# A three-block decoder layer on one core: pairs of value groups in one PSUM bank, rows of maxima ahead of the next reductions, cross queries split by GpSimd, stack reads behind the rows

## The reference, cut to what matters

```python
# x, ctx: (4, 256, 128) float32; 16 heads of 8
x = x + self_attention(layernorm(x))        # rotary q and k, causal, softmax, @ Wo.T
x = x + cross_attention(layernorm(x), ctx)  # keys and values from ctx, softmax, @ W_proj + b_proj
x = x + moe(layernorm(x))                   # per batch row: mean over tokens -> router, top 2 of 8 experts,
                                            # gelu(h @ w1[e] + b1[e]) @ w2[e] + b2[e], weighted sum
```

## Time and profile before

| | |
|---|---|
| three runs | 200.36, 200.97, 201.46 us (median 200.97) |
| profiled execution | 200.95 us, of which the span in the trace is 199.2 us |
| busy: PE, PEld, DVE, ACT, POOL | 166.8, 116.1, 140.7, 104.8, 52.3 us |
| chain that ended last, by engine | PE 50%, DVE 19%, DMA 15%, SP's queue 5%, "issue" 4%, POOL 3% |
| granted TensorE clock, mean of the span | 0.947 |

### The profile page before, as it was taken

How to read it: one execution, slowest core, us unless ns; L and a number is a source line. 1 busy time by engine, 2 the same in 40 slices (tenths; PEclk the granted TensorE clock), 3 DMA queues, 4 the chain that set the end, 5 groups by cost and what they waited for, 6 DMA issues and landing times.

```text
span 199.2 us, 4411 instructions
## 1 busy us (share of the span) xinstructions
PE 166.8 (84%) x1500; PEld 116.1 (58%) x1508; DVE 140.7 (71%) x545; ACT 104.8 (53%) x222; POOL 52.3 (26%) x103
## 2 busy tenths in 40 slices
PE   0686195699599979989998998998998899799994
PEld 0343184485466755755764655654665556598984
DVE  2789299897347899799799889888968346525020
ACT  2132021257147656566566666766676657793451
POOL 7810005668800070030030030010115107126050
PEclk9999669589769999999999999999999999999999
DMA  5817660058227503322321321300340350170720
GB/s 150 238 35 175 164 173 18 3 148 184 70 82 196 184 25 104 110 69 58 109 82 49 98 95 35 90 0 3 113 130 3 100 143 0 17 224 26 229 66 26
DMA packets 23842, 19.05 MB, mean 96 GB/s; under 512 B 2364, under 2 KB 21820, under 8 KB 23100
## 3 DMA queue, kind: packets, MB, share of 16 engines
q1 hardware_dynamic: 22908, 17.79, 31.9%
q10 hardware_dynamic: 912, 0.98, 2.0%
HBM read 12.54 MB, written 2.49 MB: 75 GB/s over the span
## 4 chain that ended last, share of the span: by engine, by line
PE 50%; DVE 19%; DMA 15%; SPq 5%; issue 4%; POOL 3%; ACT 2%; POOLq 0%; DVEq 0%; ACTq 0%
PE psV L914 11%; PE psB L893 9%; PE psA L868 8%; DMA stackQ<-maxT 6%; DMA stackQ<-scratch 4%; DVE masked L623 4%; PE psA L958 4%; PE psM L923 3%; PE psA L975 3%; DMA stackK<-hid 3%; PE psV L975 3%; PE psM L933 3%; DVE stats L554 2%; DVE negmax L629 2%; SPq L402 2%
## 5 line engine op out<-in xcount | busy, mean ns | idle before, releaser
L753 ACT ACTIVATE E<-psB 128x512 f32<-128x512 f32 x112 | 62.3, 595 | 37.3 <-PE psB L893 15.7
L868 PE MATMUL psA<-stackK,stackQ 72*128 72x256 bf16 (+1 forms) x256 | 44.4, 277 | 11.8 <-DMA stackK<-hid 5.5
L893 PE MATMUL psB<-stackQ,stackK 74*128 74x256 bf16 (+1 forms) x256 | 42.2, 264 | 4.6 <-DMA stackQ<-maxT 3.8
L623 DVE CUSTOM_DVE_ANT_0 masked<-psA,row_mask 128x128 bf16<-128x128 f32 (+1 forms) x128 | 36.8, 352 | 11.8 <-PE psA L868 11.7
L629 DVE TENSOR_REDUCE negmax<-psA 128x2 f32<-128x512 f32 x64 | 39.7, 677 | 0.0
L868 PEld LDWEIGHTS psA<-stackK,stackQ 72*128 72x128 bf16 x256 | 23.0, 105 | 21.5 <-DMA stackQ<-scratch 8.6
L914 PE MATMUL psV<-E,V 128*9 128x256 f32 (+1 forms) x512 | 30.9, 359 | 0.2 <-ACT E L753 0.2
L893 PEld LDWEIGHTS psB<-stackQ,stackK 74*128 74x128 bf16 x256 | 22.0, 100 | 12.5 <-DMA stackQ<-maxT 5.6
L468 POOL TENSOR_SCALAR rstd<-mv 128x2 f32<-128x2 f32 x12 | 2.8, 236 | 89.1 <-DVE mv L558 88.9
L914 PEld LDWEIGHTS psV<-E,V 128*9 128x9 f32 x512 | 11.0, 90 | 14.4 <-issue 7.9
L761 ACT ACTIVATE oT<-psV 128x256 f32<-128x256 f32 x32 | 12.3, 384 | 7.9 <-PE psV L914 7.2
(11 more groups left out here) (111 smaller groups left out, 247.0 us busy)
## 6 DMA issues: line engine op xcount, KB each, us to landing
stackK<-scratch SPq DMA_DIRECT2D x18, 192.0 KB
stackQ<-hid SPq DMA_DIRECT2D x36, 64.0 KB
w1s<-w_dram SPq DMA_DIRECT2D x8, 258.0 KB, 2.8
w2s<-w_dram SPq DMA_DIRECT2D x8, 256.0 KB, 3.7
stackQ<-scratch SPq DMA_DIRECT2D x3, 576.0 KB
stackK<-hid SPq DMA_DIRECT2D x18, 64.0 KB
scratch<-hid SPq DMA_DIRECT2D x4, 192.0 KB, 3.7
scratch<-parts_ctx SPq DMA_DIRECT2D x4, 192.0 KB, 4.7
```

Of the source, the lines that this page charges most:

```text
L623: last = dve.tensor_tensor_reduce(out=masked[:, bank, i * keys:(i + 1) * keys], in0=scores[:, i, 0:keys], in1=row_mask[:, S - keys:S], sca ...
L753: act.activation(dst, psB[:, bank].rearrange("p (h q) -> p h q", h=dst.shape[1]), ACT.Exp, scale=SCALE).then_inc(b_taken, 1)
L868: last = pe.matmul(psA[:, bank, i * keys:(i + 1) * keys], stackQ[0:ROWS, b, h, t * P:(t + 1) * P], stackK[0:ROWS, b, h, 0:keys], start=Tru ...
L893: last = pe.matmul(psB[:, bank, i * n:(i + 1) * n], stackK[:, b, h, t * P:(t + 1) * P], stackQ[:, b, h, q0:S], start=(s == 1 or i == 0), s ...
```

## The change

1. **Values in pairs.** `V` has 27 columns for two heads: the first head's 8 values and a 1, nine zeros, the second head's 8 values and a 1. The heads are dealt out so that group 2k has the even ones of eight, group 2k + 1 the odd ones (`heads_of`). Each group's products use 18 of the 27 columns and add into the same 18 rows of `psV`, so that two groups fill one bank. ScalarE copies it once for two groups, `o_turn` has four transposes into one bank, and VectorE divides once.
2. **Rows of maxima.** `max_rows` is cut in `max_turn` (TensorE's transpose, at the place where it was) and `max_rows` (VectorE's two instructions and SP's two transfers), which for jobs 1 to 7 stands ahead of the units of that half.
3. **Cross queries.** ScalarE copies them from PSUM to `rot`, GpSimd splits them there in four instructions, ahead of its addition of the bias.
4. **Stacks.** `stack_write` and `stack_read` are of one tensor each. Keys of batch row 2 are written from half 6 (before the rows of job 0), and read back right behind the writing of the queries; the reads of batch row 3 stand right behind the rows of job 1, ahead of the first writes of cross keys. `stack_read_k` moves from half 8j + 21 to 8j + 24.
5. **Fills.** GpSimd's memsets of `V` are two of 128 columns in place of one of 256, and a third of 128 x 9 zeros in the step `constants` of batch row 1. `masked` has two buffers in place of three.

```diff
-    put(9, "stack_write", 0, 2)
-    put(10, "stack_read", 0, 2)
-    put(14, "stack_write", 0, 3)
+    put(6, "stack_write", 0, 2, 1)
+    put(9, "stack_write", 0, 2, 0)
+    put(9, "stack_read", 0, 2, 1)
+    put(10, "stack_read", 0, 2, 0)
+    put(13, "stack_write", 0, 3, 1)
+    put(14, "stack_write", 0, 3, 0)
+    put(16, "stack_read", 0, 3, 1)
+    put(16, "stack_read", 0, 3, 0)
...
-            put(n + 2 * NG, "max_rows", s, b)
-        if j == 1:
-            put(n + 2 * NG + 1, "stack_read", 0, 3)
+            row_of[n + 2 * NG] = (s, b)
...
-            put(m, "stack_read_k", 1, b)
+            put(n + 24, "stack_read_k", 1, b)
...
+        if half in row_of:
+            order.append(("max_rows", *row_of[half]))
         order += [step for _, step in sorted(units, key=lambda unit: unit[0])]
+        if half in row_of:
+            order.append(("max_turn", *row_of[half]))
         n, h = divmod(half - LAG - 1, 2)
...
+def heads_of(g):
+
+    k, j = divmod(g, 2)
+    return [k * 2 * GH + 2 * i + j for i in range(GH)]
+
...
-        V = sb("V", [P, 2, NB, NT, NH, VC])
...
+                if kind == "stack_write":
+                    which = st["g"]
+                    sp.wait_ge((parts_q_self[b], parts_k_self[b])[which], NPART)
+                    write_parts(s, b, which, parts[:, b, which], (scr_q_self[b], scr_k_self[b])[which])
+                if kind == "stack_read":
+                    which = st["g"]
+                    sp.wait_ge((scr_q_self[b], scr_k_self[b])[which], 16)
+                    if which == 1:
+                        read_k(s, b)
+                    else:
+                        read_q(s, b)
...
-                    sp.wait_ge(misc_taken[st["misc"][0][0]], st["misc"][0][1])
+                    bank, k = use[("max_turn", s, b)][0]
+                    sp.wait_ge(misc_taken[bank], k)
...
+            v_pairs = V[:, :, :, :, :, :].rearrange("p w b t m c -> p (w b t m) c")
+            pool.memset(v_pairs[:, :, HD:VC], 1.0).then_inc(v_init, 1)
+            pool.memset(v_pairs[:, :, 3 * VC - 1:3 * VC], 1.0).then_inc(v_init, 1)
...
+                    pool.memset(v_pairs[:, :, VC:2 * VC], 0.0).then_inc(v_init, 1)
...
+                    bank, k = misc[0]
+                    pool.wait_ge(misc_taken[bank], k)
+                    split(rot[:, b % 2, 0, 0], parts[:, b, 0], parts_q[b])
...
-                if kind == "q_cross":
-                    bank, k = misc[0]
-                    dve.wait_ge(misc_full[bank], k)
-                    qq, dst = rot[:, b % 2, 0, 0], parts[:, b, 0]
-                    dve.tensor_copy(dst[:, 0], psM[:, bank, 0:S]).then_inc(parts_q[b], 1)
-                    dve.wait_ge(parts_q[b], 1)
-                    dve.tensor_tensor(qq, psM[:, bank, 0:S], dst[:, 0], ALU.subtract).then_inc(misc_taken[bank], 1)
-                    dve.wait_ge(misc_taken[bank], k)
-                    dve.tensor_copy(dst[:, 1], qq).then_inc(parts_q[b], 1)
-                    dve.wait_ge(parts_q[b], 2)
-                    dve.tensor_tensor(dst[:, 2], qq, dst[:, 1], ALU.subtract).then_inc(parts_q[b], 1)
...
-                        if unit >= NA:
-                            dve.wait_ge(a_taken, unit - NA + 1)
...
-                            last = dve.tensor_tensor_reduce(out=masked[:, bank, i * keys:(i + 1) * keys], in0=scores[:, i, 0:keys],
...
+                            last = dve.tensor_tensor_reduce(out=masked[:, unit % 2, i * keys:(i + 1) * keys], in0=scores[:, i, 0:keys],
...
-                    bank, k = misc[0]
+                    bank, k = use[("max_turn", s, b)][0]
...
-                    for t, (bank, k) in enumerate(misc):
-                        dve.wait_ge(misc_full[bank], k)
...
+                    bank, k = misc[0]
+                    dve.wait_ge(misc_full[bank], k)
+                    o = psM[:, bank].rearrange("p (n w) -> p n w", w=VW)[:, :, 0:2 * VC]
+                    o = o.rearrange("p n (j c) -> p n j c", c=VC)
+                    r = rden[:, job % 2, :].rearrange("p (n j) -> p n j", j=2)
+                    then(dve.reciprocal(r, o[:, :, :, HD]))
...
+                if kind == "q_cross":
+                    bank, k = misc[0]
+                    act.wait_ge(misc_full[bank], k)
+                    act.wait_ge(parts_q_self[2 + b] if b < 2 else parts_q[b - 2], NPART)
+                    act.activation(rot[:, b % 2, 0, 0], psM[:, bank, 0:S], ACT.Copy).then_inc(misc_taken[bank], 1)
...
-                if kind == "values":
...
-                    if g == 0 and job >= 2:
+                    if g == 1 and job >= 2:
...
+                    act.activation(oT[:, job % 2, g // 2, :], psV[:, 0:S], ACT.Copy).then_inc(v_taken, 1)
...
-                if kind == "max_rows":
...
-                        pe.wait_ge(v_init, 1)
+                        pe.wait_ge(v_init, 3)
                         pe.wait_ge(v_zeroed, 1)
-                    else:
-                        pe.wait_ge(v_taken, grp)
+                    elif g % 2 == 0:
+                        pe.wait_ge(v_taken, grp // 2)
...
+                    j = g % 2
...
+                        for i, h in enumerate(heads_of(g)):
+                            last = pe.matmul(psV[i * VW:i * VW + 2 * VC, q0:S], V[:, s, b, t, h // 2, j * VC:(j + 2) * VC],
+                                             E[:, grp % 3, i, t, q0:S], start=(j == 0 and t == 0),
+                                             stop=(j == 1 and t == 1), skip_group_check=True,
+                                             tile_position=(0, i * VW))
                     last.then_inc(v_full, 1)
...
-                        for i in range(NG):
...
+                    pe.wait_ge(v_taken, NPAIR * (job + 1))
+                    for t in range(NT):
+                        for i in range(NPAIR):
+                            last = pe.transpose(psM[:, bank, (t * NPAIR + i) * P:(t * NPAIR + i + 1) * P],
+                                                oT[:, job % 2, i, t * P:(t + 1) * P], ident[:, :])
+                    last.then_inc(misc_full[bank], 1)
```

96 lines of the change are left out of this document (41 added, 55 removed).

## The result

The changed kernel took 194.77 us in the median (four timed executions, 193.15 to 196.91) where the kernel before took 201.22 beside it; the ratio is 0.9631, with a 95% interval from 0.9577 to 0.9686. That is inside the range of the prediction and 2.9 us above its 191.9. Medians here are over all executions, but every ratio leaves out those more than 1.5% above their kernel's fastest, so this one rests on 193.15, 193.44 and a fifth execution of 193.98 us, which are 1.3 to 2.1 us above the forecast. The profiled execution of the changed kernel is the longest of these, 196.91 us; the two quickest have spans of 191.2 and 191.3 us and a mean granted clock of 0.964 where this one has 194.9 and 0.947. What part of that is the change's own and what is the clock's is the main question of what follows.

A forecast was written before the change was run, and what follows sets the result against it. It took a ring through TensorE, VectorE and SP's transfers, plus TensorE's long wait at job 2 and the low clock behind it, as the bound. Terms summed to -9.1 from 200.95, giving 191.9 us, range 189.3 to 196.3.

The forecast's parts named there:

- Stack reads: SP's queue, batch row 2: the read of keys comes 1.65 us sooner, so job 2 starts sooner; -1.65 us.
- The clock behind job 2: TensorE from 51.85 to 58.00: with a shorter wait the granted clock stays up; -2.9 us.
- Wait at job 3: TensorE at job 3: a new wait for the queries of batch row 3 where there was none; +0.75 us.
- `o_turn`: TensorE's transposes: four instead of eight save 0.46 us in each of seven jobs; -3.2 us.
- Columns: Loads of V, 9 to 18 columns: 512 loads cost between nothing and 1.5 us; +0.5 us.
- Rows of maxima first: Start of jobs: six waits for rows go (4.8 us), four cross jobs give back 0.52 each; -2.7 us.
- Ahead on one engine only: Rival: VectorE reaches reductions later and TensorE waits there instead, so the 2.7 us go; 194.6 us, chance 0.12.
- Cross queries: VectorE, four cross jobs: 1.57 us of work leaves each, mostly not TensorE's bound; -0.5 us, bounds 0 and 1.7.
- Memset: GpSimd's zeros of V at xn of batch row 1: VectorE waits for the memset's end; +0.6 us.

The follow-up runs named there:

- e10: e3 with ten products of zeros put in TensorE's wait for the queries of job 2; median 200.78 us, no ratio on record.
- e7: The kernel before with every load of V taking 18 columns and nothing else moved; median 200.28 us, ratio 0.998.
- e12: e8 with eight more zero products in a wait, and the row of maxima ahead in self jobs only, as in e9; median 190.16 us, ratio 0.952.
- e3: The changed kernel with the writes and reads of the stacks back at their old places in SP's queue; median 198.95 us, ratio 0.983.
- e5: The changed kernel with the row of maxima behind its two units and the cross queries' split back on VectorE; median 195.95 us, ratio 0.972.
- e2: The changed kernel with the row of maxima put back behind the two units that share its half; median 197.08 us, ratio 0.977.
- e11: The kernel before with only the memset of 1152 zeros added on GpSimd, into a tile not in use yet; median 202.86 us, ratio 0.997.
- e1: The changed kernel with the memset of V's zeros moved behind xn of batch row 2, about 22 us; median 193.36 us, ratio 0.956.
- e9: e1 with the row of maxima ahead of its units in jobs 1 to 3 alone, behind them in jobs 4 to 7; median 194.42 us, ratio 0.960.
- e8: e1 with 18 more warm products ahead of the first scores and twice six products of zeros in waits of job 0; median 193.44 us, ratio 0.964.

## Why the prediction was right, and where it wasn't

The total was right within its range because large misses had opposite signs, and that is luck: the row of maxima, 2.7 us of the sum, gave nothing, while the split, the stacks and the columns gave more than they were priced at.

1. **Stack reads: right.** With the row at 39.58, 2.05 us later than in the kernel before, the read of keys at 41.51 is 41.04 + 2.05 - 41.51 = 1.58 us sooner; predicted 1.65.
2. **The clock behind job 2: right.** 6.15 - 3.31 = 2.84 us for 2.9, and e10 shows that it is the clock's, apart from the wait. But e7 shows that the kernel before can come through such a wait without the fall, so over many executions the term is smaller than 2.9.
3. **Wait at job 3: too much.** The changed kernel has none over 0.3 us, e12 with its early start 0.36; predicted 0.75. Together 1 to 3 come to 5.2 us against e3 in job 2's stretch, where the prediction had 3.8. By the ratios e3 is 2.0% behind the changed kernel, 4.0 us with 1.7 us of doubt.
4. **`o_turn`: the mechanism right, the term too large.** The prediction took TensorE's whole saving as the path's. It is 0.23 us for each job beside the other changes and 0.44 without them, so 1.6 to 3.1 us in seven for 3.2. The failed step is "The division behind them is late either way, and shrinks too": it had overlapped the second four transposes.
5. **Columns: the result nearly right, the reason wrong.** Nothing for 0.5 (e7). But loads did grow, by 7 ns and not by up to 3: a load of 32 columns of other data was no measure for it. The Trainium skill ("TensorE: Matmul & The Clock Gate", LDWEIGHTS (loading the stationary operand)) puts a load at columns / 1.2 ns, so nine more columns at 7.5 ns (an estimate from it), and the trace agrees with that difference, though not with the whole of a load (91 ns at nine columns); the 3.8 us that would follow from it did not come.
6. **Rows of maxima first: the failed step.** Predicted 2.7 us over six jobs. In the five periods it loses 0.1 to 0.7 us, and it wins 0.2 to 0.3 in job 2's stretch. The fourth unit's wait is 0.87 us, as worked out. What was wrong is that the waits for rows would stay unless the row moved: from 66 to 142 us, where five of the six fell, 4.9 us of waiting in the kernel before had become 1.9 with the pairs and the new order of the stacks (e5), and 1.3 with the split off VectorE too (e2). And what the row ahead took from them came back as waits for reductions, 5.4 us for 2.1 there, where the prediction had priced 0.52 at each of four jobs. This is the rival "Ahead on one engine only", which had 0.12. That its 194.6 us lie beside the measured 194.77 is chance, since it keeps the other terms as they were forecast. What the ratios show beyond that (2.7 us, e2) is open.
7. **Cross queries: the other failed size.** Predicted 0.5, bounds 0 and 1.7; measured 1.65 to 2.19 in the periods. The prediction asked where TensorE waited long for a reduction and found nothing; the price lay in short waits (13 against 7) and perhaps in how late VectorE reached `maxT`. The fills went out 6.72 us behind `res` (118.12 - 111.40) for 6.22, 0.5 later for the 0.3 I had placed, and no cross job waited for them.
8. **Memset: the mechanism right, too small.** `xn` took 1.06 us more (1.75 for 0.69), and the first scores product was 1.1 us late in e11 (25.19 for 24.09) and 1.7 against e1, for 0.6; e7's late first product says how far one profile of it can be off. VectorE waited out both memsets, not one: 7.61 + 1.75 = 9.36 for the second's end at 9.22. The Trainium skill ("SBUF — State Buffer", Who interferes with whom) says that, when VectorE's instruction uses both its ports, whichever of the two engines issues first keeps the shared port pair for its whole instruction and blocks the other. The trace agrees that VectorE is blocked to the end and not slowed. Who issued first it doesn't show: `xn` is recorded 0.03 us ahead of the memset of zeros (7.61 for 7.64), and waited for both memsets.

Missing altogether was the clock ahead of 50 us. The prediction read the 0.50 behind job 2 and not the two stretches before it, some 7 us each in the kernel before; in the profiled execution of the changed kernel the second is 10 us long. That execution's start is 3.98 us longer. The first product's delay is 1.22 of it, and 3.3 us more at half the clock (17.0 for 13.7) are 1.6 us at most; the last 1.1 has no cause shown. e1 at 45.84 shows that nearly all of it can be absent. The same holds for the rest of the kernel: behind one wait of equal length the clock fell in the changed kernel and stayed up in e1. Timelines, the changed kernel first:

```profile
167.19 3.19 PE L1004 MATMUL psA<-w2s,hid 128*128 128x128 f32 x16 [1.19 <-ACT hid L813]
```

```profile
163.33 2.02 PE L1006 MATMUL psA<-w2s,hid 128*128 128x128 f32 x16 [1.19 <-ACT hid L815]
```

That is 53.12 us of "rest" against 51.48. Where neither happens (e1's profile) the kernel is 9.8 us shorter than before in its span, against a sum of 9.1 with and 9.7 without the memset; that profile is e1's quickest execution, and by its ratio e1 is 8.8 us shorter, with 1.1 us of doubt. Of the 2.9 us between forecast and median 1.3 (194.77 - 193.44) go with the two executions at a clock of 0.947 where the others have 0.964. By the ratio the change is worth 7.4 us (0.0369 of 200.97) with 1.1 of doubt, and the memset's missing 0.5 us with that doubt come close to the forecast 9.1. How often the long low clock comes, and why in one execution and not in another, no experiment has settled.

## What to carry over

Read the granted clock in every stretch ahead of a changed place, not only behind it: here filling three waits and one idle stretch with products that compute nothing kept it at 1.00 and gave the quickest kernel. What that alone is worth is less sure: from e9 to e12 the medians differ by 4.3 us, but the ratios by 0.8% with 1.1% of doubt, and of the 3.9 us between the two profiled spans 1.1 is at the start and 2.8 lies behind it, in e9's late row and its low clock near 167 us, which no filled wait touches. A wait that one profile names can go with whatever makes the ring shorter, so two edits against the same wait must not both be credited with it; price the second with the first in place. An edit on a full engine is paid back in many waits of some 0.3 us that no list of long waits shows, so compare periods, not waits.

## What the runs showed of the hardware

- The clock is no function of the code alone: six executions of e1 had means from 0.939 to 0.964. Behind a wait of TensorE of 2.2 to 2.5 us it fell in three profiles (before, e3, e11) and not in a fourth (e7); behind one of 1.19 us near 165 us it fell in two (changed kernel, e9) and not in five (e1, e2, e3, e8, e10). With the waits filled (e12) it was 0.99 to 1.00 over each of six executions.
- VectorE's `xn` beside two GpSimd memsets in a row, which only write, took 1.75 us for 0.69: it waited for both.
- Nine more columns in a weight load made it 91 to 98 ns, and five periods with 320 such loads 0.08 us longer.
- Two transfers of 8 KB that land in 1.8 us took up to 5.6 us with three reads of 192 KB and a writing ahead of them in the queue (e10), up to 3.6 in e3 and up to 2.0 in the kernel before, whose order is the same but whose rows come 6 to 12 us behind the reads.
